# Moving a chunked product of x between two stages of a graph kernel, and making scaled one-hots in one instruction

## The reference

```python
deg_out = clip(segment_sum(ones_e, src), 1.0)
deg_in  = clip(segment_sum(ones_e, dst), 1.0)
h   = X * rsqrt(deg_out)[:, None]
agg = segment_sum(h[src], dst) * rsqrt(deg_in)[:, None]
gX  = relu(agg @ W)
gX  = gX + relu(X @ Wres)
```

## Time and profile before

| | |
|---|---|
| median of 3 runs | 4054.07 us (4047.06 to 4056.76) |
| span of the profiled execution | 4035.4 us |
| busy: PE / DVE / ACT / POOL | 80% / 68% / 59% / 43% |
| place stage | about 233 to 546 us |
| plan stage | about 546 to 646 us |
| edges stage (convolution) | about 645 to 1209 us |

### The profile page before, as it was taken

How to read it: one execution, slowest core, us unless ns; L and a number is a source line. 1 busy time by engine, 2 the same in 40 slices (tenths; PEclk the granted TensorE clock), 3 DMA queues, 4 the chain that set the end, 5 groups by cost and what they waited for, 6 DMA issues and landing times. The chain is left out here.

```text
span 4035.4 us, 93659 instructions
## 1 busy us (share of the span) xinstructions
PE 3232.4 (80%) x25704; PEld 2882.7 (71%) x25704; DVE 2736.0 (68%) x8732; ACT 2365.9 (59%) x5642; POOL 1721.0 (43%) x1684
## 2 busy tenths in 40 slices
PE   5989945655447789956999878999749998789998
PEld 3744424555443389956998878999749988779998
DVE  9988855655448988844766546666426665458888
ACT  3779933655442278843665544666426665447888
POOL 0000044666640033345455563555454555636553
PEclk9999977876669999977999988999869999889999
DMA  0047732443219999964665433999736654328887
GB/s 18 2 163 255 254 123 64 118 103 89 77 49 372 395 330 386 386 237 131 194 189 175 146 105 106 325 325 330 268 102 191 191 175 150 115 73 258 262 261 220
DMA packets 461027, 778.11 MB, mean 193 GB/s; under 512 B 113722, under 2 KB 115898, under 8 KB 460726
## 3 DMA queue, kind: packets, MB, share of 16 engines
q1 hardware_dynamic: 379958, 594.21, 43.8%
q0 software_dynamic: 37632, 77.15, 7.5%
q10 hardware_dynamic: 43136, 102.98, 7.3%
HBM read 439.00 MB, written 334.88 MB: 192 GB/s over the span
## 5 line engine op out<-in xcount | busy, mean ns | idle before, releaser
L932 DVE SCALAR_TENSOR_TENSOR edges_acc<-edges_acc,keep,edges_ps_a 128x128 f32 (+1 forms) x2352 | 819.6, 348 | 389.5 <-issue 129.1
L900 POOL DMA_INDIRECT ring<-table_p,esrc x784 | 762.8, 973 | 626.6 <-PE edges_ps_m L1023 334.1
L1022 PE MATMUL edges_ps_m<-ring,ident 128*128 x3136 | 645.5, 287 | 143.3 <-issue 118.1
L1023 PE MATMUL edges_ps_m<-edges_q_ring,edges_turned 128*128 x3136 | 633.4, 283 | 51.3 <-issue 51.0
L917 DVE TENSOR_TENSOR edges_onehot<-iota,drel 128x512 f32<-128x512 f16 x441 | 303.2, 688 | 499.9 <-DMA table_p<-nodes_p_out 320.2
L990 ACT ACTIVATE edges_msg<-edges_ps_m 128x512 f32<-128x512 f32 x392 | 231.7, 591 | 662.8 <-DMA nodes_in_z<-table_z 226.6
L1022 PEld LDWEIGHTS edges_ps_m<-ring,ident 128*128 128x128 f32 x3136 | 497.9, 199 | 165.4 <-issue 140.0
L1023 PEld LDWEIGHTS edges_ps_m<-edges_q_ring,edges_turned 128*128 128x128 f32 x3136 | 499.2, 199 | 62.5 <-issue 61.9
L1047 PE MATMUL edges_ps_a<-ring,edges_onehot 128*128 x1568 | 307.4, 370 | 263.7 <-ACT edges_onehot L958 88.7
L1032 PE MATMUL edges_ps_a<-edges_onehot,edges_msg 128*128 128x128 f32 x3136 | 436.6, 284 | 79.3 <-issue 77.8
L1047 PEld LDWEIGHTS edges_ps_a<-ring,edges_onehot 128*128 128x128 f32 x1568 | 279.4, 272 | 291.6 <-ACT edges_onehot L958 113.5
(11 more groups left out here) (310 smaller groups left out, 7022.7 us busy)
## 6 DMA issues: line engine op xcount, KB each, us to landing
table_z<-nodes_z_t SPq DMA_DIRECT2D x196, 256.0 KB, 5.4
table_p<-nodes_p_out SPq DMA_DIRECT2D x196, 256.0 KB, 4.3
table_q<-nodes_q_out ACTq DMA_DIRECT2D x196, 256.0 KB
edges_q_ring<-table_q SPq DMA_DIRECT2D x196, 256.0 KB
edges_d_ring<-table_d ACTq DMA_DIRECT2D x98, 512.0 KB
table_t<-edges_acc SPq DMA_DIRECT2D x196, 256.0 KB
nodes_in_a<-table_t SPq DMA_DIRECT2D x196, 256.0 KB
nodes_in_z<-table_z SPq DMA_DIRECT2D x196, 256.0 KB, 4.3
```

The lines of the kernel that those rows point to most:

```text
L900: nc.gpsimd.indirect_dma_start(out=ring[:, e % RE * W:e % RE * W + P], out_offset=None, in_=table[:, :], in_offset=bass.IndirectOffsetOnAx ...
L932: nc.vector.scalar_tensor_tensor(out=to, in0=to, scalar=m.keep[:, s:s + 1], in1=ps_a[:, i % AR, where(j):where(j) + F], op0=ALU.mult, op1= ...
L1022: nc.tensor.matmul(to, m.ident[:], rows[j], start=True, stop=False)
L1023: last = nc.tensor.matmul(to, turned[:, i % QR, j * P:(j + 1) * P], slots[j], start=False, stop=True)
```

## The change

In the place stage the part of x goes away: transposes, copies, products, relus and the stores to table_r. hot_p shrinks to two of eight columns (KEEP = 2), one instruction each; for those ACT still makes val1 and val2. For the six others DVE writes val1 and val2 directly, each by one instruction that compares and multiplies (`is_equal`, then `mult`, with two scalars read per partition). The scaling of x goes from DVE (one instruction a chunk) to ACT (four activations of 128 x 128 a chunk). DVE signals once a turn, after hot_q.

In the edges stage the part of x is added: ACT's queue issues the loads of x (`load_x`) and the stores to table_r (`keep`), PE transposes after each even batch (`flip_x`) and multiplies after each odd one (`product_x`), ACT copies (`copy_x`), and DVE takes the relu as a maximum with zero (`relu_x`). The tiles ps_x and ps_r have one buffer each, and AR goes from 4 to 3. The loops run on to batch 199 and beyond so that the last chunks come out.

```diff
+XR = 4
...
-                    if g >= 1:
-                        copy_x(2 * g - 2)
-                    if g >= 2:
-                        dve.wait_ge(s_val, g - 1)
-                    nc.vector.tensor_tensor(hot_p[:, g % 2, :, :], m.iota[:, 0:P].unsqueeze(1).to_broadcast([P, SG, P]),
-                                            m.pos_low[:, g * SG:g * SG + SG].unsqueeze(2).to_broadcast([P, SG, P]), ALU.is_equal).then_inc(s_hot_p, 1)
-                    scale(2 * g)
-                    if g >= 1:
-                        copy_x(2 * g - 1)
                     if g >= 2:
                         dve.wait_ge(s_put, g - 1)
                     for u in range(SG):
                         t = g * SG + u
+                        if u < KEEP:
+                            nc.vector.tensor_scalar(hot_p[:, g % 2, u, :], m.iota[:, 0:P], m.pos_low[:, t:t + 1], None, ALU.is_equal).then_inc(s_hot_p, 1)
+                            continue
+                        for val, v in ((val1, m.v1), (val2, m.v2)):
+                            nc.vector.tensor_scalar(val[:, g % 2, u, :], m.iota[:, 0:P], m.pos_low[:, t:t + 1], v[:, t:t + 1], ALU.is_equal, ALU.mult)
+                    for u in range(SG):
+                        t = g * SG + u
                         last = nc.vector.tensor_scalar(hot_q[:, g % 2, u, :], m.iota[:], m.pos_high[:, t:t + 1], None, ALU.is_equal)
-                    last.then_inc(s_hot_q, 1)
-                    scale(2 * g + 1)
-                copy_x(NC - 2)
-                copy_x(NC - 1)
+                    last.then_inc(s_hot, 1)
...
-                    act.wait_ge(s_hot_p, g + 1)
+                def scaled(g):
                     if g >= 2:
                         act.wait_ge(s_put, g - 1)
-                    for u in range(SG):
+                    for u in range(KEEP):
                         t = g * SG + u
+                        act.wait_ge(s_hot_p, g * KEEP + u + 1)
                         nc.scalar.activation(val1[:, g % 2, u, :], hot_p[:, g % 2, u, :], ACT.Copy, scale=m.v1[:, t:t + 1])
                         last = nc.scalar.activation(val2[:, g % 2, u, :], hot_p[:, g % 2, u, :], ACT.Copy, scale=m.v2[:, t:t + 1])
-                        if g >= 2 and u % 4 == 1:
-                            relu(2 * g - 4 + u // 4)
                     last.then_inc(s_val, 1)
-                for c in range(NC - 4, NC):
-                    relu(c)
+
+                for c in range(NC):
+                    if c % 2 == 0:
+                        scaled(c // 2)
+                    k = parts(c)
+                    act.wait_ge(s_x[c % R], 16 * (c // R + 1))
+                    if c >= R:
+                        act.wait_ge(s_out[c % R], 16 * (c // R))
+                    for j in range(J):
+                        at = slice(j * D, j * D + D)
+                        nc.scalar.activation(h[0:k, c % R, at], xin[0:k, c % R, at], ACT.Copy,
+                                             scale=m.norm[0:k, 0, c * J + j:c * J + j + 1]).then_inc(s_h, 1)
...
+                    pe.wait_ge(s_hot, g + 1)
...
-    AR = 4 if degrees else QR
+    AR = 3 if degrees else QR
...
+            xin, x_t, r_out = sb("xin", [P, XR, CH]), sb("x_t", [P, 2, CH]), sb("r_out", [P, XR, CH])
+            ps_x, ps_r = pb("ps_x", 512, 1), pb("ps_r", 512, 1)
+            s_flip_x, s_x_t, s_res, s_r = sem("s_flip_x"), sem("s_x_t"), sem("s_res"), sem("s_r")
+            s_x, s_kept = [sem(f"s_x{r}") for r in range(XR)], [sem(f"s_kept{r}") for r in range(XR)]
...
+                def relu_x(c):
+                    dve.wait_ge(s_res, c + 1)
+                    if c >= XR:
+                        dve.wait_ge(s_kept[c % XR], 16 * (c // XR))
+                    nc.vector.tensor_scalar(r_out[:, c % XR, :], ps_r[:, 0, :], 0.0, None, ALU.max).then_inc(s_r, 1)
+
                 lag = 2 if degrees else BEHIND + 1
-                for i in range(NB + lag):
+                for i in range(NB + (lag + 2 if degrees else lag)):
                     if i < NB and (not degrees or i % SHARE == SHARE - 1):
                         hot(i)
-                    if i >= lag:
+                    if lag <= i < NB + lag:
                         chain(i - lag)
+                    if degrees and i >= 5 and i % 2 == 1:
+                        relu_x((i - 5) // 2)
...
-                    for i in range(NB):
-                        if i % SHARE == SHARE - 1:
-                            continue
+                    def load_x(c):
+                        if c >= XR:
+                            act.wait_ge(s_flip_x, c - XR + 1)
+                        act.dma_start(xin[0:parts(c), c % XR, :], chunk_rows(x, c)).then_inc(s_x[c % XR], 16)
+
+                    def copy_x(c):
+                        act.wait_ge(s_flip_x, c + 1)
+                        if c >= 2:
+                            act.wait_ge(s_res, c - 1)
+                        nc.scalar.copy(x_t[:, c % 2, :], ps_x[:, 0, :]).then_inc(s_x_t, 1)
+
+                    def keep(c):
+                        act.wait_ge(s_r, c + 1)
+                        act.dma_start(m.table_r[c * P:(c + 1) * P, :], r_out[:, c % XR, :]).then_inc(s_kept[c % XR], 16)
+
+                    def hot_a(i):
                         if i >= HR:
                             act.wait_ge(s_seg, i - HR + 1)
                         for j in range(4):
                             nc.scalar.activation(onehot[:, i % HR, j, :], m.iota[:, 0:P], ACT.Abs, bias=m.minus_drel[:, 4 * i + j:4 * i + j + 1]).then_inc(s_gap, 1)
                         act.wait_ge(s_gap, 4 * (i - i // SHARE) + 4)
                         nc.scalar.activation(onehot[:, i % HR, :, :], onehot[:, i % HR, :, :], ACT.Relu, bias=m.one[:], scale=-1.0).then_inc(s_hot, 1)
+
+                    for c in range(XR):
+                        load_x(c)
+                    for i in range(2 * NC + 7):
+                        if i < NB and i % SHARE != SHARE - 1:
+                            hot_a(i)
+                        if i % 2 == 1:
+                            if 0 <= (i - 3) // 2 < NC:
+                                copy_x((i - 3) // 2)
+                            if XR <= (i + 3) // 2 < NC:
+                                load_x((i + 3) // 2)
+                        elif i >= 8:
+                            keep((i - 8) // 2)
+                    for b in range(XR):
+                        act.wait_ge(s_kept[b], 16 * slot_uses(XR, b))
...
+                def flip_x(c):
+                    pe.wait_ge(s_x[c % XR], 16 * (c // XR + 1))
+                    if c >= 1:
+                        pe.wait_ge(s_x_t, c)
+                    for j in range(J):
+                        last = nc.tensor.transpose(ps_x[:, 0, j * P:(j + 1) * P], xin[:, c % XR, j * P:(j + 1) * P], m.ident[:])
+                    last.then_inc(s_flip_x, 1)
+
+                def product_x(c):
+                    pe.wait_ge(s_x_t, c + 1)
+                    if c >= 1:
+                        pe.wait_ge(s_r, c)
+                    nc.tensor.matmul(ps_r[:, 0, :], m.wres[:], x_t[:, c % 2, :], start=True, stop=True).then_inc(s_res, 1)
+
                 def batch(i):
                     if degrees:
-                        sum_rows(i)
+                        if i < NB:
+                            sum_rows(i)
+                        if i % 2 == 0 and i // 2 < NC:
+                            flip_x(i // 2)
+                        if i % 2 == 1 and i >= 3:
+                            product_x((i - 3) // 2)
                         return
                     if i < NB:
                         fetch(i)
@@ -1058,7 +1066,7 @@
                     if i < NB:
                         combine(i)
 
-                for i in range(NB + (0 if degrees else BEHIND)):
+                for i in range(NB + 2):
```

67 lines of the change are left out of this document (8 added, 59 removed).

## The result

The changed kernel takes 4019.44 us (median of five runs, 4013.94 to 4034.32) beside 4047.06 us for the kernel before (five runs, 4044.36 to 4056.76): a ratio of 0.994, interval 0.9924 to 0.9956. It is 28 us faster by the medians; 24 us were predicted. Stages are compared one by one for that reason.

What follows compares the result with a forecast made beforehand. Place was taken as full on PE, ACT and DVE, edges as a DVE chain with pauses. Place - 59 and edges + 35 gave - 24 us: median 4030 from 4054.07, own range 4000 to 4060, with rivals 3952 to 4095.

Steps and rivals of the forecast that it cites:

- Place, predicted - 59: Place stage: turns fall from 6.20 to 4.97 us with DVE the longest, saving 59 us, bounds 43 and 97.
- the clock: Place stage: a less busy PE gets a lower clock, 0.7 to 0.95; turn taken as 4.97 us, not 4.77.
- Rivals 3: Place stage: the two-pointer compare falls to hot_p's column rate; place gains only 5, total 4084 us; chance 0.06.
- 4 (free second pointer, 200): Place stage: second pointer free and clock holds; place - 97, edges + 35, total 3992 us; chance 0.07.
- Edges, predicted + 35: Edges stage: the added x work costs 5 + 5 + 25 = + 35 us, from - 60 to + 100.
- The relu: Edges stage, DVE: the 0.59 us register gap hides the 0.69 us relu; at most 10 us sticks out, 5 taken.
- PE's shorter lead: Edges stage: PE can run two batches ahead of the chain instead of three; + 0 taken for it.
- ACT's waits: Edges stage: ACT's waits for work two or more batches back cost 5 us in all.
- The pauses: Edges stage: 143 us of pauses change by + 48 if they follow PE's instructions, - 70 if halved; + 25 taken.
- rival 1: Edges stage: PE becomes the bound; from + 71 us there the kernel is slower; chance 0.25.
- Rival 2: Edges stage: the pauses shrink as PE fills; edges - 40, total 3955 us; chance 0.20.
- never over 0.192 us: Next edge stage: PE's register instructions never slow down there, cited for pauses shrinking when PE is busier.

Runs made afterwards that it cites:

- e5: The whole change as it is, run again beside the kernel before on a quiet chip; 3497.35 us beside 3553.35, ratio 0.9842.
- e7: The whole change with KEEP = 3, so three tiles in eight, not two, leave their values to ScalarE; 3480.9 us beside 3553.35, ratio 0.9797.
- e6: The place change alone, edges stage as in the kernel before, relu(x @ Wres) not computed; 3480.92 us, ratio 0.9794 to the kernel before.
- e2: The place change alone with AR = 3 instead of 4, relu(x @ Wres) left out; 3482.93 us in one run.
- e10: The whole change with PE's product of x put one batch later; 3497.57 us beside 3552.4 for the kernel before, ratio 0.9851.
- e3: As e2, with four matmuls of four columns added on PE after each batch's sums; 3482.23 us in one run.
- e8: The same kernel as e3 once more, in case another chip paused; 3481.73 us beside 3553.35 for the kernel before.
- e12: The whole change without DVE's relu in the edges stage and the product's wait for it, zeros in table_r; 3479.52 us beside 3551.73, ratio 0.9797.
- e9: The kernel before itself, unchanged, traced on a quiet chip; 3551.26 us in one run.
- e4: The whole change without POOL's gathers in this edges stage, sums using rows of old gathers; 3484.53 us in one run.

## Why the prediction was right, point by point

**Place, predicted - 59, measured - 67 to - 69.** The terms: eight hot_q 1.85 predicted, 1.86 measured; a one-pointer one-hot 0.166 and 0.163; a two-pointer one 0.216 and 0.2225; sum 4.77 and 4.86 us. The term that failed is the clock: I added 0.2 us a turn, to 4.97, on the assumption that PE at its lower rate would need 5.3 us. No run shows the 4.97. In its place the trace of after has starts 0.33 us apart where the granted clock is 0.50; sixteen of them would be 5.3 us, and no turn has sixteen. The granted clock did fall (0.85, as forecast from 0.7 to 0.95), but never for a whole turn: 20 of the 49 turns have 8 to 10 of their 16 matmuls at 0.53 us, the others have none, and no two slow turns follow one another. Six matmuls 0.165 us apart and ten 0.33 us apart are 4.3 us, still under DVE's turn. So the turn is DVE's 4.86, and 48 x (6.20 - 4.86) = 64 us plus 4 of ending. In e5 the first two turns, with up to 14 slow matmuls in one, take 5.01 and 5.20 us; there PE is the bound for a moment, and it costs 0.5 us in all. hot_p's first and last start lie 233 us apart, 239 predicted. Rivals 3 (column rate, 290) and 4 (free second pointer, 200) are refuted by the same row.

From 0.163 us at 128 columns (e7's turn above) to 0.2325 at 392 (the eight hot_q of after) it is 0.26 ns a column of f16. With the second pointer and the second operation there is a further 0.06 us, and the whole instruction, 0.2225 us, stays far below the 0.33 us of rival 3.

**Edges, predicted + 35, measured + 41 on the first chip, + 12 on the quiet ones.**
- The relu: 5 us predicted as what sticks out of the 0.59 us gap, 5.0 measured on the quiet chips outside the eighth batches. The 0.08 us on every other batch is the same on both kinds of chip (odd distances 2.184 us in the median). The unforeseen term, on the quiet chips, is the eighth batches, + 9.7 us: DVE's load of its table of slots is 0.3 us longer in e5 than in e6; on the first chip it isn't (0.598 us in the median, after). Against it stand 4.9 us that the end of the stage gives back, since POOL's pace sets it; the prediction had POOL at nothing. The gap that was to hide the relu is not always the 0.59 us of address registers, and I had read only ordinary ones. For PE's shorter lead, + 0, e2 confirms the part that AR has in it; the part of the product's wait is not isolated (e10).
- ACT's waits, 5 us: 2 us, at the last stores.
- The pauses, + 25 taken between + 48 and - 70: + 34 in the distances of over 4 us on the first chip, none on the quiet ones. PE's instructions in the stage rose by 29% (4798 to 6169), the sum in these pauses by 31% (109 to 143), which is near what "they come with the instructions" would have. That is one pair of traces; the run that was to test it (e3, e8) met no chip that pauses. On a quiet chip 38% more matmuls and weight loads cost nothing (e12, 2148 beside 1552: 451.0 us between the accumulations, 452.1 in e6).
- What the pauses look like: PE's instructions creep. In the edges stage of the first chip neighbouring starts in PE's stream (matmuls, weight loads, register instructions) lie 0.70 us apart 51 times before and 24 times after, on the quiet chips (e9, e5) not once; in DVE's and ACT's streams such a step comes at most twice in any of the four. After has plain stops too, such as 5.4 us from 1057.59 us on (inside the pause shown above) in which the trace has no instruction of PE, so creeping is not all of it. What makes PE creep or stop stays open. One rival is untested: the transfers of queue q8, which the page lists as instruction (160 of them in before, 16,384 B each), come once in about 250 instructions of PE, and in the later part of the stage (before, from 976 us on) the pauses come once in about 122, nearly half of that. A single such transfer is hardly slower on the first chip (0.99 us in the median before, 0.97 in e9), so what would have to be late is its start, and no run looked at that.
- PE as bound (rival 1): refuted. No run shows the 50 us that the range, and with it the 4095 us, put on a PE at its lower rate. PE's clock rose to 0.83 on the first chip and 0.98 on the quiet ones, and PE was busy 406 of 604 and 355 of 464 us (near 450 was forecast).
- Rival 2 (pauses shrink as PE fills): refuted on the first chip. What spoke for it was the next edge stage, where the register instructions never slow down and the clock is high. This step of the prediction failed: that stage pauses as well. It takes 718 us on the first chip and 546 on a quiet one, PE busy 587 and 530:

```profile
1768.00:2486.00 718.00, 587.08 (x4704) 562.42 (x4704) 402.09 (x981) 372.91 (x588) 380.87 (x392) 0.91 0.47 144
```
```profile
1642.00:2188.00 546.00, 529.99 (x4710) 529.65 (x4711) 404.74 (x981) 377.90 (x588) 399.10 (x395) 0.98 0.62 191
```

(Both are of the kernel before, the first on the first chip, the second, e9, on a quiet one.) PE creeps there too, only on other instructions. Three in a row, PE's lines alone, from that stage on the first chip start 0.71 and 0.69 us apart:

```profile
1854.53 0.29 PEld L1023 LDWEIGHTS edges_ps_m<-edges_q_ring,edges_turned 128*128 128x128 f32 x1 [1.81 <-issue]
1855.24 0.37 PE L1023 MATMUL edges_ps_m<-edges_q_ring,edges_turned 128*128 x1 [1.04 <-issue]
1855.93 0.29 PEld L1023 LDWEIGHTS edges_ps_m<-edges_q_ring,edges_turned 128*128 128x128 f32 x1 [1.11 <-issue]
```

In the whole stretch there are 28 such steps, in e9's none. So to look at one line's register instructions was too narrow: "never over 0.192 us" did not mean that PE never slowed down.

**The sum.** Predicted - 24 with place at - 59 and edges at + 35. By the first pair of traces it is - 69 and + 41 with + 6 of plan that the change does not own; the medians give - 28. Two errors of 10 and 6 us, of opposite sign, nearly cancelled, and the profiled pair itself differs by 4 us, not 28; that the number came so close is luck. And the number belongs to the first chip: with no pauses to lengthen, the same change is worth 56 us. The prediction named that ("if the pauses change by more than 60 us") only as a way to be wrong, not as the largest term of chance. Its whole range, 3952 to 4095 us, held the times of all four rivals too, so that the time alone could hardly have refuted it; the terms above are the test.

**What is shown and what argued.** Shown: the place gain and its bound, by e6 and e7; the end of the edges stage at POOL's pace on quiet chips, by e9 and e4; the relu with the product's wait for it as the source of the x work's cost on quiet chips, by e12; the independence of plan, by e9 and e5. Argued: that the pauses grow with PE's instructions on the first chip. Not known: what makes PE creep or stop, and what a pausing chip has that a quiet one has not. The quiet chips and the first differ only in stages in which POOL gathers (plan + 27 us, edges + 103, the two later edge stages + 175 and + 181; place, conv and nodes are equal within 4 us). That is where I would look next, with e3 and e4 repeated on a chip that pauses. e4 on a quiet chip doesn't bear on it: what goes away there is the wait for the gathers themselves.

## What to carry to other kernels

Before costing a move of work into an idle-looking stage, find out whether the idle time is a dependency's (it can be filled: 68 us more on PE, 57 on ACT and 51 MB more of transfers cost nothing here) or belongs to the chain's own engine: 0.69 us of relu in a 0.59 us gap cost the chain 5 us directly and 10 more in the gaps that hold a table load too, of which 5 came back where another engine set the pace. Cost short instructions by the distance of their starts, not by durations or by a group's length over its count: the terms of the turn came out within 3%, and the one of e7 that was taken from a group's length was off by more (0.21 for 0.163). An estimate that rests on pauses without a known cause should carry them as the main term of its range, and one run on a second chip tells whether they belong to the kernel. And a claim that an engine never slows down is to be read from all its instructions, not from one line's.

## What the runs showed of the hardware that I had not expected

- The same program takes 4047 us on one chip and 3551 on others, and the difference of the two spans, 486 us, lies in the stages with gathers (27 + 103 + 175 + 181), with the other stages equal within 4 us. On the first chip PE's instructions then come 0.70 us apart for a while, on the others never.
- POOL's gathers start 1.25 us apart, and on the quiet chips they, not DVE's chain, set the last eight or so batches of the edges stage (starts 5.05 us apart, four gathers).
- A lower granted clock cost nothing here: in place it fell from 0.99 to 0.85 when PE went from 279 of 313 to 171 of 245 us busy, and DVE's turn of 4.85 us was not touched. With KEEP = 3 the turn is 0.28 us shorter, the clock back at 0.98, and PE's busy time 141 us instead of 173 for the same 784 matmuls.
- A second pointer scalar and a second operation together cost 0.06 us a VectorE instruction (0.2225 against 0.163 us at 128 columns of f16); no run here parts the two.
- A table load into registers on DVE's queue takes 0.60 us in the median (e6), and 0.91 in e5, where the relu stands in the same gap; but 0.60 on the first chip and in e10 with the relu there too, and 0.84 in e4. What decides is not known.
